# Attention and mixture-of-experts block on one core: normalisation, statistics, scale and x loads of the projection stage in another order

## The reference

```python
x = x + _layernorm(_L0_attn_ref(_layernorm(x, axis=-1), ...), axis=-1)
x = x + _layernorm(_L0_ffn_ref(_layernorm(x, axis=-1), ...), axis=-1)
return x
```

```python
def _layernorm(x, axis=-1, eps=1e-05):
    m = jnp.mean(x, axis=axis, keepdims=True)
    v = jnp.var(x, axis=axis, keepdims=True)
    return (x - m) / jnp.sqrt(v + eps)
...
q = (x @ Wq).reshape(b, s, 2 * H, hd)
k = (x @ Wk).reshape(b, s, 2 * NUM_KV_HEADS, hd)
v = (x @ Wv).reshape(b, s, NUM_KV_HEADS, 2 * hd)
q = rope(q).transpose(0, 2, 1, 3) * scaling
k = rope(k).transpose(0, 2, 1, 3)
```

## Time and profile before

| | |
|---|---|
| median of 3 runs | 5983.11 us (5982.58 to 5988.96) |
| the profiled execution | 5986.48 us |
| its span | 5984.7 us |
| projection stage | 0 to about 466 us |
| attention | about 466 to 5390 us |
| the stages after it | about 5390 us to the end |
| busy in the projection stage, of 466 us | PE 373.3, DVE 334.6, ACT 287.0, POOL 375.3 |

### The profile page before, as it was taken

The page is one execution under the profiler, slowest core; times in us unless marked ns, Lnnn a source line. Parts: engine busy times, 40 slices in busy tenths (PEclk is TensorE's granted clock), DMA queues, the critical chain, the costliest instruction groups (busy, mean ns, idle before and its releaser), DMA issues. The chain is left out here.

```text
span 5984.7 us, 167689 instructions
## 1 busy us (share of the span) xinstructions
PE 5595.3 (93%) x50896; PEld 1969.1 (33%) x50896; DVE 5495.3 (92%) x6072; ACT 4976.3 (83%) x9206; POOL 2070.0 (35%) x3655
## 2 busy tenths in 40 slices
PE   8878999999999999999999999999999999987776
PEld 4541333333333333333333333333333333325424
DVE  7868999999999999999999999999999999967716
ACT  6665999999999999999999999999999999973314
POOL 7981222222222222222222222222222222225406
PEclk9997999999999999999999999999999999998878
DMA  5671222232232222222222222222232222206588
GB/s 179 205 207 47 53 52 53 52 52 52 53 51 54 52 51 54 50 53 51 50 51 52 51 53 52 53 53 53 52 52 53 52 51 53 53 16 202 198 364 276
DMA packets 436838, 495.27 MB, mean 83 GB/s; under 512 B 132051, under 2 KB 298099, under 8 KB 428003
## 3 DMA queue, kind: packets, MB, share of 16 engines
q1 hardware_dynamic: 435171, 485.74, 33.4%
q10 hardware_dynamic: 1024, 0.53, 0.0%
HBM read 360.60 MB, written 123.21 MB: 81 GB/s over the span
## 5 line engine op out<-in xcount | busy, mean ns | idle before, releaser
L741 DVE TENSOR_REDUCE at_largest<-at_ps_m 128x1 f32<-128x1024 f32 x4096 | 4695.8, 1210 | 44.2 <-PE at_ps_m L845 31.6
L707 ACT ACTIVATE at_e<-at_ps_e 128x512 f32<-128x512 f32 x8192 | 4407.0, 597 | 356.7 <-PE at_ps_e L814 156.1
L831 PE MATMUL at_ps_o<-at_e,at_v 128*32 128x256 f32 (+1 forms) x30720 | 2680.3, 421 | 33.4 <-ACT at_e L707 21.4
L845 PE MATMUL at_ps_m<-k_stack,q_stack 48*128 48x512 bf16 x8192 | 2484.3, 384 | 87.7 <-DVE at_largest L741 55.6
L814 PE MATMUL at_ps_e<-q_stack,k_stack 51*128 51x512 bf16 x8192 | 2514.5, 382 | 8.1 <-issue 2.4
L831 PEld LDWEIGHTS at_ps_o<-at_e,at_v 128*32 128x32 f32 x30720 | 845.2, 149 | 1559.3 <-issue 818.0
L814 PEld LDWEIGHTS at_ps_e<-q_stack,k_stack 51*128 51x128 bf16 x8192 | 566.7, 93 | 1665.7 <-ACT at_e L707 1628.7
L626 POOL TENSOR_TENSOR at_negated<-at_zeros,at_largest_t 128x32 f32<-128x32 f32 x256 | 64.9, 254 | 2160.8 <-DVE at_largest_t L748 2160.8
L845 PEld LDWEIGHTS at_ps_m<-k_stack,q_stack 48*128 48x128 bf16 x8192 | 572.8, 93 | 219.4 <-DVE at_largest L741 189.0
L669 POOL TENSOR_TENSOR at_rms<-at_mean_eps,at_minus_half 128x16 f32<-128x16 f32 x128 | 372.8, 2912 | 10.0
L645 POOL TENSOR_TENSOR at_crossed<-at_totals 128x32 f32<-128x32 f32 x128 | 32.4, 253 | 756.6 <-DMA at_totals<-at_sums 756.6
(11 more groups left out here) (132 smaller groups left out, 3012.5 us busy)
## 6 DMA issues: line engine op xcount, KB each, us to landing
k_stack<-k_parts SPq DMA_DIRECT2D x1536, 64.0 KB
q_stack<-q_parts SPq DMA_DIRECT2D x256, 192.0 KB
q_stack<-q_parts SPq DMA_DIRECT2D x256, 128.0 KB
w_first<-in_w SPq DMA_DIRECT2D x32, 1024.0 KB, 23.3
ex_w_second<-in_w SPq DMA_DIRECT2D x32, 1024.0 KB, 26.0
q_parts<-pr_parts SPq DMA_DIRECT2D x96, 256.0 KB, 2.5
k_parts<-pr_parts SPq DMA_DIRECT2D x96, 256.0 KB, 2.8
pr_x_in<-in_x SPq DMA_DIRECT2D x16, 1024.0 KB, 5.7
```

The lines of the kernel that those rows point to most:

```text
L707: nc.scalar.activation(e[:, j % E_BUFS], ps_e[:, bank(u, j)], ACT.Exp, scale=SCALE).then_inc(exp_done, 1)
L741: nc.vector.reduce_max(largest[:, u % 2, j // SIDE, j % SIDE:j % SIDE + 1], ps_m[:, j % 2], AX.X).then_inc(max_done, 1)
L831: last = nc.tensor.matmul(ps_o[32 * tile:32 * tile + 32, columns], v[:, u, tile // 2, first:first + 2 * VD * TILES - kt:TILES], e[:, (QUAD ...
L845: last = nc.tensor.matmul(ps_m[:, j % 2, half * HALF:(half + 1) * HALF], q_stack[rows, u, pair, c, t * P:(t + 1) * P], k_stack[rows, u, pa ...
```

## The change

Seven edits, all in `project`:

1. SP: `load(n + 3)` moves from ahead of the stores of chunk 0 to ahead of the stores of chunk 2, that is behind both q chunks' stores and the v store.
2. DVE: `statistics(n + 2)` moves from the end of slot 2 to the end of slot 1.
3. DVE: two new operations of 128x8 elements after the aggregation: the negated mean and the variance plus epsilon.
4. POOL: `scale` keeps the power and one product (`neg_mean` times `rstd`); the addition of epsilon and the subtraction from zero go, and with them two constant tiles.
5. ACT: `normalise` is cut in halves of four tiles, at the head of slots 0 and 1 of the batch before.
6. ACT: the four transposed copies are cut in two pairs, at the head of slots 2 and 3.
7. Semaphore counts follow: `xn_ready` rises twice a batch, and PE's transposes wait for the half that they read.

```diff
             w = sb("w", [P, KC, 3, D])
-            eps, minus_half, zeros = sb("eps", [P, TILES]), sb("minus_half", [P, TILES]), sb("zeros", [P, TILES])
+            minus_half = sb("minus_half", [P, TILES])
             x_in = sb("x_in", [P, 2, TILES, D])
...
             var, rstd = sb("var", [P, TILES]), sb("rstd", [P, TILES])
-            shift, bias = sb("shift", [P, TILES]), sb("bias", [P, TILES])
+            neg_mean, bias = sb("neg_mean", [P, TILES]), sb("bias", [P, TILES])
             xn = sb("xn", [P, TILES, D])
...
             v_stored = [sem("v_stored0"), sem("v_stored1")]
-            dve_step, pool_step, passed = sem("dve_step"), sem("pool_step"), sem("passed")
+            dve_step, pool_step, passed, pool_passed = sem("dve_step"), sem("pool_step"), sem("passed"), sem("pool_passed")
             x = io["x"].rearrange("b (t p) d -> b p t d", p=P)
...
                 def load(n, u):
-                    sp.wait_ge(xn_ready, n - 1)
+                    sp.wait_ge(xn_ready, 2 * (n - 1))
                     sp.dma_start(x_in[:, u], x[bass.ds(n, 1)].rearrange("o p t d -> (o p) t d")).then_inc(x_loaded[u], 16)
...
                 def batch(n, u, more):
-                    if more:
-                        load(n + 3, 1 - u)
                     for ch in range(CHUNKS):
+                        if ch == 2 and more:
+                            load(n + 3, 1 - u)
                         scr = self.q_scr if ch < KC else self.k_scr
...
             def _(pool):
-                nc.gpsimd.memset(eps[:], EPS).then_inc(pool_set, 1)
                 nc.gpsimd.memset(minus_half[:], -0.5).then_inc(pool_set, 1)
-                nc.gpsimd.memset(zeros[:], 0.0).then_inc(pool_set, 1)
                 nc.gpsimd.memset(ones[:], 1.0).then_inc(ones_set, 1)
-                pool.wait_ge(pool_set, 3)
+                pool.wait_ge(pool_set, 1)
                 pool.wait_ge(ones_set, 1)
...
                     pool.wait_ge(var_done, m + 1)
-                    nc.gpsimd.tensor_tensor(var[:], mean_var[:, :, 1], eps[:], ALU.add).then_inc(pool_step, 1)
-                    pool.wait_ge(pool_step, 3 * m + 1)
                     if not (isinstance(m, int) and m == 0):
-                        pool.wait_ge(xn_ready, m)
+                        pool.sem_inc(pool_passed, 1)
+                        pool.wait_ge(xn_ready, 2 * m)
                     nc.gpsimd.tensor_tensor(rstd[:], var[:], minus_half[:], ALU.pow).then_inc(pool_step, 1)
-                    pool.wait_ge(pool_step, 3 * m + 2)
-                    nc.gpsimd.tensor_tensor(shift[:], mean_var[:, :, 0], rstd[:], ALU.mult).then_inc(pool_step, 1)
-                    pool.wait_ge(pool_step, 3 * m + 3)
-                    nc.gpsimd.tensor_tensor(bias[:], zeros[:], shift[:], ALU.subtract).then_inc(rstd_done, 1)
+                    pool.wait_ge(pool_step, m + 1)
+                    nc.gpsimd.tensor_tensor(bias[:], neg_mean[:], rstd[:], ALU.mult).then_inc(rstd_done, 1)
...
-                def normalise(m, u):
+                def normalise(m, u, side):
                     act.wait_ge(rstd_done, m + 1)
                     if not (isinstance(m, int) and m == 0):
-                        act.wait_ge(t_done, TILES // 2 * m)
-                    for t in range(TILES):
+                        act.wait_ge(t_done, KC * (2 * m - 1 + side))
+                    for t in range(side * TILES // 2, (side + 1) * TILES // 2):
                         last = nc.scalar.activation(xn[:, t], x_in[:, u, t], ACT.Identity, bias=bias[:, t:t + 1],
...
                     c = CHUNKS * n + ch
-                    if ch == 3 and more:
-                        for j in range(4):
+                    if ch < 2 and more:
+                        normalise(n + 1, 1 - u, ch)
+                    if ch >= 2 and more:
+                        for j in range(2 * (ch - 2), 2 * (ch - 1)):
                             copy_transposed(n + 1, 1 - u, j)
...
                                    ps_v[:, ch % 2].rearrange("p (k m) -> p k m", k=2)).then_inc(v_copied, 1)
-                    if ch == 0 and more:
-                        normalise(n + 1, 1 - u)
...
-                normalise(0, 0)
+                for side in range(2):
+                    normalise(0, 0, side)
                 for j in range(4):
...
                     last.then_inc(dve_step, 1)
-                    dve.wait_ge(dve_step, m + 1)
+                    dve.wait_ge(dve_step, 2 * m + 1)
                     if not (isinstance(m, int) and m == 0):
...
                         last = nc.vector.bn_aggr(mean_var[:, t], stats[:, t])
-                    last.then_inc(var_done, 1)
+                    last.then_inc(dve_step, 1)
+                    dve.wait_ge(dve_step, 2 * m + 2)
+                    nc.vector.tensor_scalar(neg_mean[:], mean_var[:, :, 0], -1.0, None, ALU.mult)
+                    nc.vector.tensor_scalar(var[:], mean_var[:, :, 1], EPS, None, ALU.add).then_inc(var_done, 1)
...
                         leave_out(c - 2, (ch - 2) % RING)
-                    if ch == 2 and more2:
+                    if ch == 1 and more2:
                         statistics(n + 2, i + 1, u)
...
                 def transposes(m, banks):
-                    pe.wait_ge(xn_ready, m + 1)
                     for j in banks:
+                        if j % KC == 0:
+                            pe.wait_ge(xn_ready, 2 * m + j // KC + 1)
                         pe.wait_ge(t_copied, 4 * m + j - 1 + 2)
```

## The result

| | before | after |
|---|---|---|
| median | 5982.84 us (5981.39 to 5988.96, 4 runs) | 6050.05 us (6045.39 to 6052.91, 4 runs) |
| the profiled execution, its span | 5986.48, 5984.7 us | 6052.91, 6051.1 us |
| ratio | | 1.0103 [1.0091, 1.0115] |

The changed kernel is slower by 67 us; +52 was forecast, and 6050 lies inside the range of 6010 to 6062. The mechanism came as described. The price of one batch was set about 1.2 us too low (31.17 us measured, 30.0 forecast).

The account below looks back on a forecast made before the run. Bound by a ring of handovers in the projection stage, which the late x load lengthens from 25.83 to 30.0 us: 12 batches at 4.2 us (50), the last +3, ends gaining about 1, +52, median 6035 us; range 6010 to 6062.

Parts of the forecast that it names:

- What bounds it: Projection stage: handovers between engines; after the change DVE's statistics wait for x about 5 us in each of 13 batches.
- Step 1: DVE, from the statistics' start to slot 2's first product: statistics, aggregation, two small operations of 0.1 us each; together 3.75 us.
- port wait: Rival, chance 0.10: DVE's two small operations wait 2.1 us for POOL in each batch; period 32.1 us, total 6061.
- Steps 2 and 3: DVE's products, then POOL's slot 3 additions and third parts: first addition at 9.5 us, last third part ends at 19.3.
- Step 4: SyncE: v store issued 2.47 us after the last third part, the load about 0.45 later, at about 22.3 us.
- the ring: Load lands, statistics, products, additions, third parts, q stores, v store, next load: 30.0 us a batch instead of 25.83.
- Step 5: Landing of x behind v: v lands 5.4 us after issue, x 2.7 to 3.6 later, at 29.9 to 30.8; 30.0 taken.
- The sum: Whole stage: 12 intervals of 4.2 us make 50, the last +3, first and last batches gain about 1: +52 us.
- the meeting at full clock: DVE's rest meeting POOL's last third part if TensorE's clock stays full: another 1.0 us, period 31.0; left out.
- What the other edits give back: Shorter scale and normalisation halves: worth nothing in the new ring; without it POOL's operations and DVE's rests need 24.1 us.
- faster: Rival, chance 0.05: x is in time, POOL and the rests decide at 24.1 us a batch; -24 us, 5959.
- The clock: TensorE starts at clock 0.50 after its stall, so the next q ends about 2.3 us later; steps 1 to 5 unaffected.

Follow-up runs that it names:

- the two kernels at 29.3 and 29.6: Kernel before with only the x load moved behind the v store: 6029.76 us; changed kernel with the statistics back in slot 2: 6030.26 us.
- the first experiment: Changed kernel with only the x load put back at the head of SyncE's batch, ahead of the q stores: 5955.89 us, 0.9933.

## Why the prediction was right, and where its size was off

- **What bounds it.** Right. DVE waits for x; less the 10.6 us of two such waits in the prologue (10.8 in the kernel before), it is 86.7 us in 13 batches (60 or more forecast). It is 10.8 us in the first of them, 8.6 in the last and 5.2 to 6.9 in the others. The experiment with the load back at the head takes the whole loss away.
- **Step 1, the small operations.** Right at 0.17 and 0.16 us. These two rows are what rules out the *port wait* rival: by the numbers alone its 32.1 us a batch and 6061 us lie nearer to the measured 31.17 and 6050 than the 30.0 and 6035 of the forecast. The port wait is real, but not here: POOL's queue is dry. With the load in time POOL is not dry:

```profile
269.40 0.86 DVE L375 TENSOR_SCALAR pr_neg_mean<-pr_mean_var 128x8 f32<-128x8 f32 x1
```

  This is DVE with the load at the head of the batch, under a third part of POOL from 268.09 to 270.23; with the load between the q chunks it is 1.60 us at 296.77, under an addition from 295.99 to 298.35, and up to 2.26 us elsewhere. The 0.86 and the 1.60 us both end when POOL ends. The Trainium skill's rule (SBUF — State Buffer, "SBUF: two separate sides"), one holder of the port pair for a whole instruction, agrees with these two. The rule is for a DVE operation in a 2-port mode; no run shows the mode of this one.
- **Steps 2 and 3.** Right to 0.16 us, the meeting of rest and first addition (3.25 us) included.
- **Step 4.** The load is issued 0.68 us behind v, 0.45 were assumed, and 22.56 us into the ring, 0.26 later than forecast.
- **Step 5, the term that was mis-sized.** The distance from v's landing to x's was right: 2.8 us were taken out of the 2.7 to 3.6 of the working, and it is 2.9 (337.51 + 6.1 = 343.6, 338.19 + 8.3 = 346.5). What was wrong is the landing of v itself. The 5.4 us came from stores with nothing queued right behind them; with x behind it v lands in 6.0 to 6.2 us. That is 0.7 of the 0.8 us by which this step misses. Together with step 4 it is 1.0 us of the ring. The upper end of the working, 30.8, would have come nearer, but for a reason that the trace does not show.
- **The sum.** Twelve regular batches lost 63.5 us (eleven 58.9, the next 4.6) where 50 were forecast: this is nearly the whole miss of 14 us. The other ends cancel: the last three intervals +4.9 for +3, the first batch -2.7 for about -1. That 31.2 us lie close to the 31.0 which the prediction names for the meeting at full clock is chance: the clock fell, and that meeting did not take place.
- **What the other edits give back.** Right that they are worth nothing in this ring, shown by the two kernels at 29.3 and 29.6. The bound of 24.1 without the ring was 0.8 too high, because it lets POOL's scale and DVE's rests exclude each other. They don't, as the last section shows: 24.1 less one rest of 1.13 is 23.0, and 23.26 is measured. The *faster* rival, 5959 at 0.05, is what the first experiment gave (its ratio times 5983 is 5943), but only with the load moved back; as a case of this change it had no chance.
- **The clock.** Right for this kernel: it falls, costs q 2.35 us, and that is off the ring. With the load in time or nearly so it is on the path. In the kernel with the whole normalisation it costs 1.6 to 1.7 us a batch (27.0 against 25.35 after the same gap); with the load between the q chunks its share is not separated from the port's.

Open: a third x buffer, which would let the load go out earlier wherever it stands, was not tried. That near k stores lengthen the load's landing is read from four kernels (k stores 2.6, 2.6, 3.6 and 6.8 us behind it, from load to statistics about 9.4, 9.5, 9.4 and 8.5 us), not tested by itself. How much halves and pairs bring with the statistics in slot 2 and the load early was not run, and the two were undone only together. The shorter scale was not undone by itself with the load in time.

## What to carry to other kernels

A load in an in-order queue starts no earlier than the last store ahead of it. Before moving it, count from the issue to the reader on today's timetable (15.4 us in hand here), take off both moves (15.0 and 7.6), and if the rest is negative, add up the ring. A landing measured with nothing behind it is too short for a transfer with another one queued right behind: here 5.4 us became 6.1. An edit that gains nothing beside one bad edit can still be the gain: undo the parts one at a time before giving up the whole. Where TensorE has gaps of some microseconds on the path, look at the granted clock behind each, and compare the batches in which it fell with those in which it held: removing a gap of 2.7 us, and the slow clock behind it, was worth 3.4 us a batch here. A version that keeps TensorE busy is no clean test of the clock once TensorE's own work sets the pace.

## What the runs showed of the hardware that was not expected

- The issue of the x load on SyncE right behind the 1 MB v store takes 1.83 to 1.96 us in the kernel after, where it stood alone 0.40 to 0.43. The engine's queue is held that long. It is not so behind every 1 MB transfer: with the order turned round, the issue of the v store right behind the x load takes 0.42 to 0.46 us. What makes the difference is not shown.
- Behind a gap of TensorE of 2.69 or 2.87 us the 1.2 GHz level can follow, but need not: behind 2.69 us it fell in nine batches and held in two of the kernel with the whole normalisation, behind 2.87 us it fell with the load between the q chunks and held with the load ahead of the v store (q in 3.70 us at 276.50).
- A DVE operation of eight elements a partition that takes 0.17 us alone takes up to 2.39 us when it starts with or under an addition or third part of POOL.
- POOL's power operation and DVE's rest run side by side at full speed. POOL and DVE of the kernel with the load at the head:

```profile
252.38 1.64 POOL L253 TENSOR_TENSOR pr_rstd<-pr_var,pr_minus_half 128x8 f32<-128x8 f32 x1
```

```profile
252.60 1.21 DVE L381 TENSOR_TENSOR pr_rest<-pr_rotated,pr_parts 128x1024 f32<-128x1024 f32 x1
```

  An addition or third part makes the rest take up to 3.29 us, the power doesn't: 1.65 and 1.22 us are what they take alone, and all 13 such meetings of this kernel show the same (1.21 to 1.22 us for the rest). The rule of the Trainium skill (SBUF — State Buffer, "SBUF: two separate sides") has a GpSimd operation that reads SBUF hold the pair for its whole length against a DVE operation with two SBUF inputs; here the measurement differs.
- TensorE kept busy by repeated work is no sure way to hold the clock: with 40 matmuls in place of 8 it still fell in three of eleven stalls, after gaps of 3.2 to 3.8 us behind them, and held after another gap of 3.24.
